# Values stored per key tile in the first stage; first attention loads issued by GpSimd, all later ones by SP; attention bias read in place

## The reference

```python
x = x + conv(_ln_c(x))                       # _ln_c: layernorm over the 256 channels
# conv, on pixels (B, H, W, C):
qkv = xh @ w_qkv.T + b_qkv                   # q scaled by 32 ** -0.5
attn[b, n, h, w, i, j] = q[b, n, h, w] . k[b, n, ri[h, i], ci[w, j]] + rpb[n, bih, biw]
out = softmax(attn over the 49 neighbours) @ v of the same neighbours
out = out @ w_proj.T + b_proj
```

```python
t = t + ffn(_ln_t(t))                        # top 2 of 8 experts, softmax of their gate logits
```

## Time and profile before

| | us |
|---|---|
| median of 3 runs | 1283.79 |
| lowest and highest | 1280.42, 1288.73 |
| the profiled execution | 1292.44 |
| its span, first to last instruction | 1290.6 |
| stage A, its loop and tail with compute | 0 to about 158 |
| no compute between the stages | about 158 to 173 |
| stage B | about 173 to 460 |
| stages C and E | about 460 to 1290 |

### The profile page before, as it was taken

The page is one execution under the profiler, slowest core; times in us unless marked ns, Lnnn a source line. Parts: engine busy times, 40 slices in busy tenths (PEclk is TensorE's granted clock), DMA queues, the critical chain, the costliest instruction groups (busy, mean ns, idle before and its releaser), DMA issues. The chain is left out here.

```text
span 1290.6 us, 38314 instructions
## 1 busy us (share of the span) xinstructions
PE 1139.3 (88%) x12145; PEld 966.3 (75%) x12146; DVE 922.6 (71%) x3165; ACT 637.3 (49%) x1306; POOL 757.3 (59%) x818
## 2 busy tenths in 40 slices
PE   3999849999999979971299999999999999999995
PEld 2667538999999858761288888888888888888884
DVE  7878559999999959975266666666666666666662
ACT  3566538999999937752133333333333333333331
POOL 6321248666666616777356566666666666666655
PEclk9999959999999979975599999999999999999997
DMA  6878977787787659996212323322233332232322
GB/s 164 244 234 254 260 178 185 187 205 186 190 206 196 171 167 355 370 314 208 79 23 48 50 42 50 51 49 47 47 44 49 50 50 47 46 51 42 51 48 29
DMA packets 155175, 169.87 MB, mean 132 GB/s; under 512 B 17274, under 2 KB 146954, under 8 KB 154706
## 3 DMA queue, kind: packets, MB, share of 16 engines
q1 hardware_dynamic: 112480, 126.32, 35.1%
q0 software_dynamic: 21920, 29.38, 13.6%
q10 hardware_dynamic: 20706, 13.34, 4.3%
HBM read 108.36 MB, written 65.49 MB: 135 GB/s over the span
## 5 line engine op out<-in xcount | busy, mean ns | idle before, releaser
L1607 ACT ACTIVATE e_gf<-e_ps_h,keep_b 128x256 f32<-128x256 f32 x448 | 212.2, 474 | 415.1 <-PE e_ps_h L1554 415.1
L1554 PE MATMUL e_ps_h<-e_xt,w1s 128*128 128x256 f16 x2688 | 323.0, 275 | 5.6 <-PEq L1546 4.2
L1554 PEld LDWEIGHTS e_ps_h<-e_xt,w1s 128*128 x2688 | 249.3, 98 | 72.4 <-issue 38.5
L1569 PE MATMUL e_ps_y<-w2s,e_g_hi 128*128 x1792 | 296.4, 273 | 0.0
L1569 PE MATMUL e_ps_y<-w2s,e_g_lo 128*128 x896 | 244.2, 273 | 0.0
L958 POOL TENSOR_TENSOR b_p<-b_s,b_p 128x392 f16<-128x392 f32 x196 | 182.8, 933 | 86.0 <-DVE b_p L813 82.2
L1507 POOL DMA_INDIRECT out<-e_y,e_xg x112 | 185.3, 1654 | 80.3 <-POOLq L1504 44.7
L1630 DVE TENSOR_TENSOR e_g_lo<-e_gf,e_g_hi 128x256 f16<-128x256 f32 x448 | 208.9, 466 | 15.4
L1569 PEld LDWEIGHTS e_ps_y<-w2s,e_g_hi 128*128 128x128 f16 x1792 | 173.1, 98 | 19.0
L1628 DVE CAST e_g_hi<-e_gf 128x256 f16<-128x256 f32 x448 | 146.9, 328 | 23.4 <-ACT e_gf L1607 23.4
L898 ACT ACTIVATE b_s<-b_s,b_neg_max 128x196 f32<-128x196 f32 x392 | 158.2, 454 | 5.4 <-DVE b_neg_max L795 2.8
(11 more groups left out here) (145 smaller groups left out, 1590.3 us busy)
## 6 DMA issues: line engine op xcount, KB each, us to landing
h_v<-v_rows SPq DMA_DIRECT2D x196, 99.5 KB
e_xg<-slots SPq DMA_DIRECT2D x56, 273.0 KB, 2.8
a_w_in<-in_w SPq DMA_DIRECT2D x16, 512.0 KB, 4.0
c_w_in<-in_w SPq DMA_DIRECT2D x16, 512.0 KB, 8.9
v_rows<-a_v SPq DMA_DIRECT2D x14, 455.0 KB, 6.5
a_x<-in_x SPq DMA_DIRECT2D x14, 448.0 KB, 6.0
qk_hi<-a_o_hi SPq DMA_DIRECT2D x14, 448.0 KB, 4.8
qk_lo<-a_o_lo SPq DMA_DIRECT2D x14, 448.0 KB, 5.7
```

Source lines behind the costliest of these rows:

```text
L1554: mm = pe.matmul(ps_h[:, hc % 4, 0:ST], w1s[:, bass.ds(e, 1), w, a:a + 128].rearrange("p a n -> p (a n)"), xt[:, s, :, 2 * p + k, :], star ...
L1569: mm = pe.matmul(ps_y[:, s, h * C:(h + 1) * C], g[:, s, hc, h * 128:(h + 1) * 128], w2s[:, bass.ds(e, 1), w, a:a + C].rearrange("p a n -> ...
L1607: act.activation(gf[:, hc % 4, :], ps_h[:, hc % 4, 0:ST], ACT.Gelu, bias=b1_sb[:, bass.ds(e * HC + hc, 1)], scale=1.0 / WSCALE).then_inc(g ...
```

## The change

- A value row is stored once for each key tile that has it. `v_rows` becomes `v_tiles` (7 tiles x 112 image rows x 14 pixels x 520). SP's one store per group becomes 14: for each of 7 tiles, and for even and odd image rows apart, 14 partitions with 4 rows of 1040 bytes each. With 14 x 14 of 56 pixels per row, 784 rows per group are stored instead of 448.
- The two halves of a tile's keys are now 7 image rows of 14 pixels each, so that a value load is one block of 98 rows in DRAM. Keys are read in plain order.
- The loads for image 0's first band (13 transfers), the two query masks and the identity go from SP to POOL, between its last splits. All 14 value loads of that band stand on SP between the stores of the second-last and the last group.
- The second copy of the keys goes from ACT to SP everywhere, and `qk_used2` with its waits goes.
- `table` and its 36 copies go; the instruction that adds the bias reads a 14 x 14 window of `bias`.

The core of the diff:

```diff
-    grid = v_rows.rearrange("(b h w) c -> b h w c", b=B, h=H)
     for j in range(2):
-        at = key_col(t) + j * HCOL
-        queue.dma_start(ht["v"][:, t, j, :], grid[s, bass.ds(r0, KR), at:at + HCOL, :]).then_inc(ht["v_in"][t], 16)
+        queue.dma_start(ht["v"][:, t, j, :], v_tiles[t, bass.ds(s * H + r0 + j * KC_ROWS, KC_ROWS)
+                                                     ].rearrange("r w c -> (r w) c")).then_inc(ht["v_in"][t], 16)
...
                     sp.wait_ge(v_out, s + 1)
-                    sp.dma_start(v_rows[bass.ds(tok, BAND), :].rearrange("(t p) c -> p t c", p=QT),
-                                 v_sb[:, s].rearrange("p (t h) d -> p t (h d)", t=TPG)).then_inc(stored_v[s], 16)
+                    for t in range(COLS):
+                        for odd in range(QT // W):
+                            at = odd * W + key_col(t)
+                            sp.dma_start(v_tiles[t, bass.ds(row, QR), :, :].rearrange("(a p) w c -> p w a c", p=QT // W)[odd],
+                                         v_sb[at:at + KCOL, s].rearrange("p (t h) d -> p t (h d)", t=TPG)
+                                         ).then_inc(stored_v[s], 16)
...
-                step(0, (GROUPS - 4) * BAND, E - 1, False)
-                load_keys(sp, ht, qk_hi, qk_lo, 0, 0)
-                sp.wait_ge(ht["q_clear"], 2)
-                for h in range(2):
-                    load_keys_again(sp, ht, qk_hi, 0, 0, h)
-                load_mask(sp, ht, k_mask, 0, 0)
-                step(1, (GROUPS - 3) * BAND, E - 1, False)
+                step(0, (GROUPS - 4) * BAND, (GROUPS - 4) * QR, E - 1, False)
+                step(1, (GROUPS - 3) * BAND, (GROUPS - 3) * QR, E - 1, False)
...
-                step(0, (GROUPS - 2) * BAND, None, False)
-                for t in range(2, 5):
-                    load_values(sp, ht, v_rows, 0, t, 0)
-                step(1, (GROUPS - 1) * BAND, None, False)
-                for t in range(5, COLS):
-                    load_values(sp, ht, v_rows, 0, t, 0)
+                step(0, (GROUPS - 2) * BAND, (GROUPS - 2) * QR, None, False)
+                for t in range(COLS):
+                    load_values(sp, ht, v_tiles, 0, t, 0)
+                step(1, (GROUPS - 1) * BAND, (GROUPS - 1) * QR, None, False)
...
-                with pool.Fori(0, GROUPS // 2) as i:
+                with pool.Fori(0, GROUPS // 2 - 3) as i:
                     for s in range(2):
                         split_w1(s, i + 1)
+                load_keys(pool, ht, qk_hi, qk_lo, 0, 0, ht["first_in"])
+                for s in range(2):
+                    split_w1(s, E - 3)
+                load_mask(pool, ht, k_mask, 0, 0, ht["first_in"])
+                pool.wait_ge(ht["q_clear"], 2)
+                load_queries(pool, ht, qk_hi, qk_lo, 0, 0, ht["first_in"])
...
-                        in1=table[:, r_cls, t_cls, hp, :], scale=-1.0, scalar=3.0e38, op0=ALU.add, op1=ALU.min,
+                        in1=bias[:, hp, y:y + KR, xx:xx + KCOL], scale=-1.0, scalar=3.0e38, op0=ALU.add, op1=ALU.min,
...
-                        if k in (0, 2) and not first:
-                            load_keys_again(act, ht, qk_hi, 1, r0, k // 2)
-                        if k in (SPS, SPS + 2) and not last:
-                            load_keys_again(act, ht, qk_hi, 0, r0_next, (k - SPS) // 2)
```

More of the change, by code:

```diff
@@ L230, in load_w1, with step @@
                                                  ].rearrange("p a n -> p (a n)")).then_inc(w1_ld[s], 16)
-                def step(s, tok, e, more):
+                def step(s, tok, row, e, more):
                     if more:
@@ L599, in stage_b @@
         pt_sb = sb("b_pt", [CK, 4, 8, LANES], F16)
-        table = sb("b_table", [LANES, 3, 3, HP, KEYS], F32)
         neg_max = sb("b_neg_max", [LANES, RING, 2], F32)
@@ L706, in _, with scores @@
                 pe.sem_inc(o_free, 2)
-                def scores(j):
+                def scores(j, opens):
                     s, t = j // SPS, j // SPT % COLS
-                    if j % SPS == 0:
+                    if j == 0 and opens:
+                        pe.wait_ge(ht["first_in"], 13 * 16)
+                    elif j % SPS == 0:
                         pe.wait_ge(band_in[s], 13 * 16)
@@ L769, in pair @@
                             pe.wait_ge(m_ok, 2 * (k - 4) + 2)
-                        band_done = scores(k) if k < STEPS else False
+                        band_done = scores(k, first) if k < STEPS else False
                         if va is not None:
@@ L775, in pair @@
                         if va is not None:
-                            values(va, (qk_used, qk_used2) if band_done else ())
+                            values(va, (qk_used,) if band_done else ())
                     for q, n in used.items():
@@ L801, in _, with pair @@
                     dve.sem_inc(stored[t], 32)
-                def pair(r_cls, first, last):
+                def pair(off, first, last):
                     used = {q: 0 for q in (p_ok, o_ok, norm, scaled)}
@@ L908, in store, with pair @@
                                   ).then_inc(stored[t], 16)
-                def pair(r, r0, r0_next, first, last):
+                def pair(r, first, last):
                     used = 0
@@ L936, in pair @@
                     act.sem_inc(t_ok, -used)
-                for h in range(2):
-                    load_keys_again(act, ht, qk_hi, 1, 0, h)
-                pair(0, 0, QR - HALF, True, False)
-                with act.Fori(1, BANDS - 2) as r:
-                    pair(r, r * QR - HALF, (r + 1) * QR - HALF, False, False)
-                pair(BANDS - 2, (BANDS - 2) * QR - HALF, H - KR, False, False)
-                pair(BANDS - 1, H - KR, None, False, True)
+                pair(0, True, False)
+                with act.Fori(1, BANDS - 1) as r:
+                    pair(r, False, False)
+                pair(BANDS - 1, False, True)
             @block.gpsimd
@@ L959, in pair @@
                                                ALU.subtract).then_inc(lo_ok, 1)
-                            if first and used <= len(spreads):
-                                copy = spread_one(pool, *spreads[used - 1])
-                                if used == len(spreads):
-                                    copy.then_inc(table_ok, 1)
                     pool.sem_inc(hi_ok, -used)
```

124 lines of the change are left out of this document (52 added, 72 removed).

## The result

| | before | after |
|---|---|---|
| median, us | 1286.08 (4 runs) | 1317.72 (4 runs) |
| lowest and highest | 1280.42, 1288.73 | 1314.15, 1318.50 |
| profiled execution, its span | 1292.44, 1290.6 | 1314.15, 1312.3 |

The ratio is 1.0244, 95% interval 1.0219 to 1.0270: slower, by 31.6 us between the medians. The forecast was 1312 us, with a range from 1290 to 1345.

A forecast was written before the change was run, and what follows sets the result against it. The prediction took stage A to go at its engines' pace, the joint at SP's queue and stage B at DVE's; with 14 stores SP binds stage A. +30.4 - 0.9 - 0.9 = +28.6 us gave 1312 us, range 1290 to 1345.

The forecast's parts named there:

- Stage A bound by SP: Stage A loop: 14 value stores make SP's queue the bound, 11.9 us per group against 9.37 before.
- my lowest bound of 0.52: Stage A loop: least cost of one value store on SP, 0.32 us issue plus 0.20 us gap; rival's chance 13%.
- my 0.45: SP's value stores: assumed issue time of one 14-partition store, 0.45 us, without the gap.
- The narrow split: SP's value stores: 14 partitions don't split over 16 engines, costing perhaps 0.07 to 0.2 us more per issue.
- L893's 0.55 against L892's 0.48: Two loads in the rows of before: the one-partition load's longer issue was taken as a sign of a narrow split's cost.
- What L128 has more than L104: Value load against key load, 0.5 us: forecast put part to the narrow split, the rest to mismatched source blocks.
- The tail: SP's queue at the end of stage A: stage B opens at 203.6 instead of 173.25, +30.4 us.
- The transfers as a rival: Stage A loop: transfers bind, not issues, once one holds its engines over 0.40 us; about +13 more, 1325 us; 10%.
- Key copies from ACT to SP: Stage B: nothing in the band loop because SP has room; -0.9 us at the start, before ACT's first exponential.
- Bias in place: Stage B: reduction's window costs nothing, DVE's 12 copies only shift a wait, removing POOL's 24 gives -0.9 us.
- the difference of two tiles: Stage B: a tile takes 2.86 us during POOL's copies and 2.76 later; over some nine tiles -0.9 us.
- The sum: Whole kernel: +30.4 - 0.9 - 0.9 = +28.6 us, median 1312 us.

The follow-up runs named there:

- the run with values first: Changed kernel with each group's 14 value stores issued ahead of its q/k stores instead of behind them: 1310.90 us, ratio 1.0201 to the kernel before.
- the two runs above: Changed kernel with a single value store per group, plus either one wide store to an unused place (1295.72 us) or 14 small ones (1350.54 us).
- the one with the table: Changed kernel with the bias table and its 36 copies of before kept: 1320.27 us, ratio 1.0264 to the kernel before.
- the spread run: Changed kernel with a single value store, second key copies back on ACT, first band's value loads spread over stage A's tail: 1278.59 us, ratio 0.9939.
- one store alone: Changed kernel with the single value store per group and the value layout of before: 1290.66 us, ratio 1.0038 to the kernel before.

## Why the prediction held, and where not

- **Stage A bound by SP, 11.9 us per group.** Right: 11.87 (nine groups from 40.69 to 147.54), without a wait. That the store's price fitted so well is luck: two errors cancel. The usual issue is 0.32 us, not 0.45; with gap it costs 0.50, under my lowest bound of 0.52. The first three of 14 take 0.9 us in the mean, behind the q/k stores, which I had not seen at all. The mean of all 14 is 0.455, next to my 0.45. The 14 with gaps come to 8.9 us where I had 9.1, and what SP does besides to 3.0 where I had 2.8.
- **What in the rows of before pointed to it.** The single value store of 1.15 us stood in the same place, right behind the q/k stores, and I took nothing from it. How much of the 1.15 is its place no run shows; the run with values first moved only the 14.
- **The narrow split** costs nothing at issue: 0.320 us at the median, against 0.316 for the shortest key load. L893's 0.55 against L892's 0.48 was not a sign of it: after, the same two take 0.55 and 0.68. The rule of the Trainium skill's page "DMA: Bandwidth & Descriptors" (section "Why a DMA increments its semaphore by 16 and not by 1"), by which the sequencer itself writes what is missing of 16, leaves no time in these rows, 0.320 against 0.316. What L128 has more than L104 is its mismatched blocks alone: the same 98 partitions take 0.32 us from a plain block and 0.77 to 0.81 from rows of 14 or 7 pixels.
- **The tail.** I had the opening at 203.6, it came at 204.42, again by terms that cancel. The tenth group's stores start 1.5 us earlier than forecast and take 0.5 less; the next four groups' take 1.6, 1.9, 0.3 and 1.5 us more than 7.0 each, for the long ones; the value loads take 0.9 less; and from the last issue to the opening it is 2.1 us instead of 3.7. -1.5 - 0.5 + 5.3 - 0.9 - 1.6 = +0.8.
- **The transfers as a rival.** Not the bound of the loop, by the two runs above. Their size stands in the trace's DMA packets, of which the values' alone have 1040 bytes in the loop. In its stretch (41.90 to 133.50) such a packet takes 72.7 ns in the mean after (6267 of them), and 55.9 before (4480). A store has 56: 4.07 us of engine time, which is 0.25 us of all 16 engines, or 0.29 of 14, the number of the prediction. The forecast let this rival begin at 0.40. The Trainium skill's page "SBUF — State Buffer" (section "Door 1") gave an estimate of 0.53 by its ports. The trace has the engines held for about half of that; how long one store lasts from its first byte to its last was not read. The rival stood close behind SP all the same: a share of 0.85 over 11.87 us is 10.1 us of the DMA engines per group, more than the 9.37 of before. So with the issues for nothing the loop might still not have been back (an estimate from this one run).
- **Key copies from ACT to SP.** The price, 0, came out in the sum, but its reason was wrong, and that is luck too. In the kernel before SP has no room; moved there alone, the copies cost 11.3 us of stage B. They are free here because another part of the change, the value loads as plain blocks, gives SP room; the prediction didn't link the two. At the start the two issues gave about what I said: the first exponential comes 6.79 us behind the opening instead of 7.87, -1.1 against -0.9.
- **Bias in place.** -1.8 to -2.0 (changed kernel against the one with the table, the spread run against before) where I had -0.9. The mechanism was right, the size too small. The reduction stayed at 0.36, as forecast. The 12 copies on DVE only shift its wait for ACT, as forecast: the first cast comes 7.62 us behind the opening without them and 7.66 with them. POOL's copies make DVE's casts longer, 1.3 to 1.6 us in all where I had 0.9 from the difference of two tiles. The last 0.5, in the last pair, is in no term of mine.
- **The sum.** The opening moved by +31.2 and stage B by -3.1, +28.1 against my +28.6. The medians stand 31.6 apart. From the start of stage C to the end, which the change doesn't touch, the profiled execution of before took 828.7 us, that of after 822.2, and those of the runs on the two chips of like speed 822.7 to 824.8. So the two profiled executions differ by 21.7 us only, and the 3.5 us by which the medians differ more than the stages are left to the variation from run to run.

## What to carry to other kernels

Count issues, not bytes, on the queue that has to send them, and ask the waits of that queue for its slack in every stage: an engine whose busy time isn't in the table can be full. A layout that makes many cheap loads out of dear ones is worth its price only where the queue that loads is the bound and the queue that stores isn't; here it bought room in stage B, which the kernel before got by giving four issues per pair to ACT. And a change of several parts should be split: the parts that gain here (the bias in place, the first loads on GpSimd and the tail's order) are together worth 0.6%, while the change as a whole costs 2.4%. Last, compare two kernels at more than one point of a stage: with the table the first reduction came 1.8 us later, but the first cast at the same time, and the loss was made behind it.

## What the runs showed of the hardware that I had not expected

- An issue's length depends on what stands ahead of it in the queue. The same store is 0.32 us further on and 0.9 us in the mean (0.32 to 1.36) as one of the first three behind two 448 KB stores; put in that place, a w1 load went from 0.38 to 0.82 and 1.02 us. Why it is mostly three, and what is waited for, no run shows.
- An issue with matching blocks takes 0.32 us and one with mismatched blocks 0.77 to 0.81 (medians), all of them with 98 partitions on one side; a 14-partition store of whole rows takes 0.32 too. In the tail of stage A, which is written out without address registers, the same store takes 0.39 with a gap of 0.04, in the loop 0.32 with a gap of 0.18.
- DVE's cast of the first tiles takes 0.75 us, and 0.84 while POOL copies 128 x 196 pieces of the bias between its own work.
- Small stores aren't cheaper to issue than large ones: median 0.319 us at 7 KB against 0.320 at 57 KB.
- The DMA engines can run at a share of 0.99 and 296 GB/s while compute keeps nearly its pace (PE busy for 83.84 us of the stretch, 83.48 with one store alone); the cost shows only where the loop ends (8 us at the opening).
- PE's granted clock in the loop of stage A fell with its busy time, from 1.00 at 85.85 us to 0.93 at 74.47: for a part of it PE ran at the lower of its two levels, 1.2 instead of 2.4 GHz. In the stretch without work between the stages it is 0.50, the lower level throughout.
